# The fourth stage of a decoder kernel on one core: x added by TensorE and copied by ScalarE, three of sixteen triangles weighted on ScalarE, another order at the loop's ends

## What is computed

```python
phi = k_val[..., None] * theta                     # k_val (b, l, 32, 8), theta 8 values
re_k, im_k = (jnp.cos(phi), jnp.sin(phi))
merged = jnp.concatenate([p_w, pw5 * re_k, pw5 * im_k], axis=-1)    # p_w: a weight per head and row
cs = jnp.cumsum(merged, axis=1)                    # den, num_re, num_im
state_re, state_im = num_re / den, num_im / den    # inv_den = 1 / max(den, 1e-4)
out_re = jnp.sum(state_re * q_re + state_im * q_im, axis=-1)
out_im = jnp.sum(state_im * q_re - state_re * q_im, axis=-1)
y = out_re @ W_re + out_im @ W_im                  # per head, 8 -> 48
y = y_val * silu(y_gate)
x = x + y @ W_out
```

## Time and profile before

| what | value |
|---|---|
| median of three runs (lowest, highest) | 1734.25 us (1733.59, 1737.01) |
| profiled execution, its own time | 1731.17 us |
| its span, first to last instruction | 1729.4 us |
| mean granted TensorE clock | 0.965 of full speed |
| busy in the span: PE, PEld, DVE, ACT, POOL | 91%, 73%, 61%, 49%, 39% |
| the loop of the fourth stage | from 1028.2 us to 1332.7 us, 304.5 us |
| of it, steps 9 to 31, in which all parts run | from 1099.0 us |

### The profile page before, as it was taken

One profiled execution on the slowest core, in us unless ns is written; L12 is line 12 of the kernel. 1 busy time (PEld: TensorE's weight loads), 2 busy tenths in 40 slices (PEclk: granted clock), 3 DMA queues, 4 the chain that ended last, 5 costly groups with the idle time before them and its releaser, 6 DMA issues. The chain is left out here.

```text
span 1729.4 us, 37862 instructions
## 1 busy us (share of the span) xinstructions
PE 1577.0 (91%) x15048; PEld 1270.1 (73%) x15048; DVE 1056.8 (61%) x1671; ACT 849.3 (49%) x1466; POOL 678.7 (39%) x527
## 2 busy tenths in 40 slices
PE   6999999999997887898999787999996898999998
PEld 4788888888885665776888464666664675888887
DVE  5757666766666887676432659999994574111121
ACT  3545455545552665655422356667672674222222
POOL 0212212212222563531422256999994431223322
PEclk9999999999997997999999798999999898999999
DMA  3111201202113100001010120000001900000000
GB/s 106 37 45 53 80 27 52 79 27 67 63 46 114 58 2 26 10 12 23 26 68 39 44 49 2 1 2 2 2 2 39 359 10 1 1 13 13 1 12 13
DMA packets 72353, 70.29 MB, mean 41 GB/s; under 512 B 24816, under 2 KB 64368, under 8 KB 71840
## 3 DMA queue, kind: packets, MB, share of 16 engines
q1 hardware_dynamic: 72224, 68.46, 12.4%
HBM read 46.03 MB, written 19.27 MB: 38 GB/s over the span
## 5 line engine op out<-in xcount | busy, mean ns | idle before, releaser
L1503 DVE TENSOR_TENSOR s6f_hid<-s6f_act_sb,s6f_u_ps 128x512 f32<-128x512 f32 x64 | 44.0, 687 | 218.2 <-PE s6f_u_ps L1454 218.2
L1526 POOL TENSOR_TENSOR s6f_hid_parts<-s6f_hid,s6f_hid_parts 128x512 fp32r<-128x512 f32 x64 | 82.7, 1292 | 223.3 <-ACT s6f_hid_parts L1492 223.3
L712 DVE TENSOR_TENSOR x_rows<-x_rows,s_o_ps 128x1024 f32<-128x1024 f32 x64 | 78.0, 1219 | 135.2 <-PE s_o_ps L612 135.2
L2243 POOL TENSOR_TENSOR s4b_with_q<-s4b_with_q 128x1024 f32<-128x1024 f32 x64 | 150.9, 2384 | 0.9 <-DVE s4b_with_q L2198 0.9
L2198 DVE TENSOR_TENSOR s4b_with_q<-s4b_c_ps,s_q_rows 128x2048 f32<-128x2048 f32 x64 | 146.0, 2284 | 2.2 <-PE s4b_c_ps L2337 2.2
L667 ACT ACTIVATE s_zT<-s_z_ps,s_bias 128x512 fp32r<-128x512 f32 x64 | 44.1, 689 | 150.0 <-PE s_z_ps L603 150.0
L612 PE MATMUL s_o_ps<-s_w_parts,s_zT 128*128 128x256 f32 x768 | 110.1, 294 | 4.6 <-DVE s_zT L693 4.6
L2535 POOL TENSOR_TENSOR s1q_halves<-s1q_full,s1q_halves 128x768 fp32r<-128x768 f32 x16 | 33.3, 2084 | 200.6 <-ACT s1q_halves L2523 200.6
L1492 ACT ACTIVATE s6f_hid_parts<-s6f_hid 128x512 fp32r<-128x512 f32 x64 | 40.5, 632 | 143.8 <-PE s6f_o_ps L1474 140.5
L543 PE MATMUL s_v_ps<-s_wv_parts,s_xnT 128*128 128x256 f32 x768 | 104.0, 285 | 1.9 <-PEq L283 1.4
L1474 PEld LDWEIGHTS s6f_o_ps<-s6w_parts,s6f_hid_parts 128*128 128x128 f32 x768 | 99.1, 188 | 6.6 <-issue 1.0
(11 more groups left out here) (332 smaller groups left out, 3886.6 us busy)
## 6 DMA issues: line engine op xcount, KB each, us to landing
stored_weights<-s1q_halves SPq DMA_DIRECT2D x16, 768.0 KB, 3.9
s6w_parts<-stored_weights SPq DMA_DIRECT2D x32, 384.0 KB, 7.3
s1q_packed<-in_codes SPq DMA_DIRECT2D x8, 384.0 KB, 4.9
s1q_scale<-in_scale_rows SPq DMA_DIRECT2D x8, 384.0 KB, 5.4
s3p_raw<-in_ffn_pieces SPq DMA_DIRECT2D x8, 384.0 KB, 9.1
early_values<-s_vbd SPq DMA_DIRECT2D x1, 2176.0 KB, 12.0
s_vbd<-early_values SPq DMA_DIRECT2D x4, 544.0 KB, 7.2
x_rows<-in_x SPq DMA_DIRECT2D x4, 512.0 KB, 5.4
```

The costliest lines, as they stand in the source:

```text
L712: nc.vector.tensor_tensor(core.x[:, t0:t0 + TG, :], core.x[:, t0:t0 + TG, :], o_ps[:, :, :].rearrange("p b (t n) -> p (b t) n", t=2), ALU. ...
L1503: nc.vector.tensor_tensor(hid[:, f % 2, :], act_sb[:, f % 2, :], u_ps[:, f % 2, :], ALU.mult) \
L1526: nc.gpsimd.tensor_tensor(hid_parts[:, f % 2, 1, :], hid[:, f % 2, :], hid_parts[:, f % 2, 0, :], ALU.subtract).then_inc(low_done, 1)
L2243: nc.gpsimd.tensor_tensor(with_q[:, half, :, 0, :, n_, :], with_q[:, half, :, 0, :, n_, :], with_q[:, half, :, 1, :, 1 - n_, :], op).then_ ...
```

## The change

Within the steps in which all parts run:

- VectorE's `add` goes. TensorE's `output` now begins with a matmul of x with the identity, so that the sum of x and of the six old products stands in PSUM, and ScalarE's `write_back` copies it to x. It has lag 8 as `add` had; it stands in ScalarE's list behind `sines` and before `yT_copy`, and it now gives `added`.
- GpSimd weights 13 of the 16 triangles; the other three are three operations of ScalarE between the sine and the absolute value, with the weight as a scale read per row. `running_sums` waits for both.

At the ends: the reciprocal of `den` is taken in two halves in step 0 and not whole in step 1; a Silu of one column before the loop loads the table; for the first units `sines` stands before `rounding(0)`, and for units 2 and 3 `phases` and `fraction` stand behind the sums and the products. In the last steps VectorE takes the scaling of units 30 and 31, the subtraction and the product with the gate of unit 31. The last turns and outputs go to the free banks of `turns_ps` and `c_ps`, and their order is written out by hand.

```diff
@@ VectorE
+                        if isinstance(u, int) and u == 0:
+                            tiles = slice(n_ * NT // 2, (n_ + 1) * NT // 2)
+                            nc.vector.reciprocal(inv_den[:, tiles, :], den[:, tiles, :]).then_inc(inverted, 1)
...
-                run_steps(dve, UNITS, [(reduce, 4), (add, 8), (fraction(0), 0), (products(0), 2),
-                                       (fraction(1), 0), (products(1), 2), (gather_stats, 8)])
+                run_steps(dve, UNITS, [(within(LAST, UNITS, combine_last), 4), (reduce, 4),
+                                       (within(LAST - 1, UNITS, scale_late), 4), (within(LAST, UNITS, multiply_last), 5),
+                                       (within(0, 2, fraction(0)), 0), (within(4, UNITS, fraction(0)), 0),
+                                       (products(0), 2), (within(2, 4, fraction(0)), 0),
+                                       (within(0, 2, fraction(1)), 0), (within(4, UNITS, fraction(1)), 0),
+                                       (products(1), 2), (within(2, 4, fraction(1)), 0), (gather_stats, 8)])
@@ GpSimd
-                run_steps(pool, UNITS, [(multiply, 6), (scale, 5), (weight, 1), (combine, 3)])
+                run_steps(pool, UNITS, [(within(0, LAST, multiply), 6), (within(0, LAST - 1, scale), 5),
+                                        (weight, 1), (combine, 3)])
@@ ScalarE
+                def write_back(u, i, half):
+                    if half == 0:
+                        return
+                    act.wait_ge(o_full, i + 1)
+                    nc.scalar.activation(core.x[:, i, :], output_of(u, i), ACT.Copy).then_inc(added, 1)
...
+                    for k in range(OWN, HK):
+                        nc.scalar.activation(tri_p[:, half, k, :], tri_seq, ACT.Copy,
+                                             scale=p_rows[:, i, half * HK + k:half * HK + k + 1]) \
+                            .then_inc(weighted_here, 1)
...
+                nc.scalar.activation(afrac[:, 0:1], core.c("half_pi"), ACT.Silu)
+                run_steps(act, UNITS, [(within(0, LAST - 1, gates), 6), (within(0, 3, sines), 1), (rounding(0), 0),
+                                       (within(3, UNITS, sines), 1), (within(0, LAST - 3, write_back), 8), (within(0, LAST - 2, yT_copy), 6),
+                                       (within(0, LAST - 1, outT_copy), 5),
+                                       (rounding(1), 0), (cosines, 1)], head=UNITS + 8)
+                outT_copy(30, 15, 0)
+                gates(30, 15, 0)
+                yT_copy(29, 14, 1)
+                outT_copy(31, 15, 1)
+                gates(31, 15, 1)
+                yT_copy(30, 15, 0)
+                write_back(29, 14, 1)
+                yT_copy(31, 15, 1)
+                write_back(31, 15, 1)
@@ TensorE, turn_outs
-                    wait(pe, added, i - 1)
+                    wait(pe, added, min(i, LAST // 2 - 1) - 1)
@@ TensorE, output
+                    nc.tensor.matmul(output_of(u, i), core.c("ident"), core.x[:, i, :], start=True, stop=False)
                     for c in range(6):
-                        last = nc.tensor.matmul(o_ps[:, D:2 * D], yT[:, i % 2, c // 3, c % 3, :], w_out[:, c, :],
-                                                start=(c == 0), stop=(c == 5))
+                        last = nc.tensor.matmul(output_of(u, i), yT[:, i % 2, c // 3, c % 3, :], w_out[:, c, :],
+                                                start=False, stop=(c == 5))
```

More of the change, by code:

```diff
@@ L1808, in stage_L1_attention @@
     UNITS = 2 * NT
+    LAST = UNITS - 1
     ROUND = 12582912.0
@@ L2161, in upto, with within, guarded @@
                 return min(n, most) if isinstance(n, int) else n
+            def within(first, to, part):
+                def guarded(u, i, half):
+                    if (first <= u < to) if isinstance(u, int) else to - first > UNITS // 2:
+                        part(u, i, half)
+                return guarded
             def q_view(i, half):
@@ L2172, in by_bank, with turned_y, output_of @@
                 return rows.rearrange("p (a k) n -> p a k n", a=2)
+            def turned_y(u):
+                if isinstance(u, int) and u >= LAST - 2:
+                    return turns_ps[:, 0:3 * P]
+                return y_ps[:, 0, 0:3 * P]
+            def output_of(u, i):
+                if isinstance(u, int) and u >= LAST - 4:
+                    n = i - (LAST - 4) // 2
+                    return c_ps[:, n // 2, n % 2, 0:D]
+                return o_ps[:, D:2 * D]
             @block.vector
@@ L2234, in weight @@
                     nc.gpsimd.tensor_tensor(
[L2235 to L2237 removed]
+                        tri_p[:, half, 0:OWN, :], tri_seq.unsqueeze(1).to_broadcast([P, OWN, S]),
+                        p_rows[:, bass.ds(i, 1), half * HK:half * HK + OWN].rearrange("p t k -> p (t k)")
+                        .unsqueeze(2).to_broadcast([P, OWN, S]), ALU.mult).then_inc(weighted, 1)
                 def combine(u, i, half):
                     pool.wait_ge(prod_done, 2 * (u + 1))
[L2242 removed]
+                    last = isinstance(u, int) and u == LAST
+                    for n_, op in ((0, ALU.add), (1, ALU.subtract))[:1 if last else 2]:
                         nc.gpsimd.tensor_tensor(with_q[:, half, :, 0, :, n_, :], with_q[:, half, :, 0, :, n_, :],
@@ L2355, in heads @@
                     pe.wait_ge(oT_out, u + 1)
-                    wait(pe, yT_out, u)
+                    if u < LAST - 1:
+                        wait(pe, yT_out, u)
+                    else:
+                        pe.wait_ge(gated, u)
                     for part in range(2):
```

67 lines of the change are left out of this document (46 added, 21 removed).

## The result

| | before | after |
|---|---|---|
| median of the runs, us | 1733.92 (1733.47 to 1737.01, 4 runs) | 1771.09 (1770.82 to 1771.63, 4 runs) |
| profiled execution, its time and span, us | 1731.17, 1729.4 | 1771.09, 1769.3 |
| mean granted clock | 0.965 | 0.950 |
| first `phases` to the start of the next stage, us | 305.6 | 340.4 |

The change makes the kernel slower, clear of the noise: ratio 1.0196, 95% interval 1.0167 to 1.0225, so the loss lies between 1.7% and 2.2%. The prediction was 1763.8 us, range 1748 to 1778.

The account below looks back on a forecast made before the run. The prediction took a two-step ring of waits through TensorE, ScalarE and VectorE (16.90 us) as the bound. Terms 4.9 + 25.6 + 6.4 - 0.4 - 7.0 = +29.5 us gave 1760.7, plus 3.1 for the median: 1763.8 us, range 1748 to 1778.

Parts of the forecast that it names:

- The predicted ring: Closed chain of waits through TensorE, ScalarE and VectorE over two steps: 7.74 + 3.84 + 5.32 = 16.90 us before the change.
- The odd leg: Odd step, ScalarE's first rounding to VectorE's second fraction: from 3.84 to 5.97 us.
- term (3): Odd steps: write_back gives added, so TensorE waits for ScalarE's copy before turn_outs; +2.13 us each, 12 times, +25.6 us.
- Terms (1) to (3): Steady steps: x's matmul on TensorE +4.9 us; three triangles on ScalarE and its late copy together +25.6 us.
- w: Time of ScalarE's three triangles together in a step: 0.72 us, with ends at 0.16 and 1.20.
- Term (4): Steady steps: GpSimd saves 3/16 of each weighting and VectorE the add, neither on the ring: 0.
- Term (5): Granted clock falling after TensorE's new stand in odd steps: 4 falls of 1.6 us, +6.4 us, bounds 0 and 19.
- The ends: Loop's start -0.4 us (bounds -2 and +1); loop's end net -7.0 us (bounds -12 and -2).
- A: Faster: VectorE is the bound, a pair takes 16.1 us, 1717 us in all; 7%.
- B: No change: the wait is half as long and the ends give -12, 1734 us; 3%.
- C: Predicted chain with the clock kept, its term at 0: 1757 us; hardly a fall had 35%.
- D: Predicted chain with the clock down in every pair, its term at 19: 1777 us; most falling had 15%.

Follow-up runs that it names:

- e3: Changed kernel with ScalarE's copy of x at the head of its step and all 16 triangles on GpSimd; 1729.67 us.
- e1: Changed kernel with ScalarE's copy of x at the head of its step, before the first rounding; 1747.72 us.
- e2: Changed kernel with all 16 triangles weighted on GpSimd and none on ScalarE, copy of x left in place; 1748.87 us.
- e6: Changed kernel with ten unused matmuls on constants ahead of turn_outs in odd steps from the fifth on, to keep TensorE busy; 1755.63 us.
- e4: Changed kernel with only its new loop ends: VectorE adds x as before for tiles 0 to 12, all triangles on GpSimd; 1725.84 us.
- e13: Kernel of e4 with odd-step output between first phases and running sums, second phases and rounding earlier, and three triangles on ScalarE; 1723.49 us.
- e5: Changed kernel with six of 16 triangles weighted on ScalarE in place of three; 1786.68 us.

## Why the prediction was right, point by point

**The direction and the chain.** The predicted ring was right in each leg. The odd leg was to be 5.97 us and is 6.01; x's matmuls were to add 0.41 and add 0.44; the pair was to take 19.44 and takes 19.51 undisturbed. In the signs that the prediction named: the stand of 2 to 2.7 us in front of `turn_outs`, ended by the copy, is 2.23; VectorE's wait of over 2 us is 2.40; its share was to be 83%, and is 79% with the falls. One sign was off: from the reduction of unit 31 to the last statistics it was to be about 7 us shorter, and is 5.6 (20.0 to 14.4). e3 shows that nothing else of the moved work counts, and e1 and e2 that the two causes inside term (3) are 1.47 and 0.70 us.

**Terms (1) to (3).** 4.9 + 25.6 = 30.5 us predicted; 28.7 + 2.2 = 30.9 measured. w, which the trace of before did not show, was put at 0.72 us from the rows of operations with a scale from a tile, and the triangles' step is 1146.76 - 1146.04 = 0.72. The bounds of 0.16 and 1.20 were not needed. The Trainium skill's figure for a pointer operand ("ScalarE: Activation LUTs", What ACT_TABLE_LOAD costs), by which it would be the same 0.72, agrees with this row.

**Term (4)** was zero, and is: VectorE's busy time fell from 16.48 us a pair (164.83 / 10) to 16.21 (162.10 / 10) and GpSimd's from 16.24 to 15.49, and the pair did not heed it. The 16.59 us of the single pair at 1144.51 is no measure of it, since its stretch takes in 12 operations and the next one 11.

**Term (5), the clock, was mis-sized.** I took 4 falls of 1.6 us, 6.4. Four full ones between step 9 and step 31 cost 1.92 us each, and the first two pairs are 0.7 us long each, at a granted clock of 0.92. The fall in step 31 costs 1.15 in the odd leg and, by e6, 1.75 behind it. Together that is 7.7 + 1.4 + 1.15 + 1.75 = 12.0 us, the whole by which e6's stage is shorter. The price of one fall is 1.15 us in the odd leg (0.46 in `turn_outs`, where I had 0.2, and 0.69 in `phases`, as reckoned), 0.63 from the odd step's second fraction to the next (0.54 of it VectorE's wait for the sums; I had 0.7 for them), and 0.14 from there on, where TensorE comes late from the heads, which took 2.44 and not 1.56. The number of falls was a guess between none and all, and that four of the eleven pairs had a full one is luck. The runs show that falls go with the stand (e6) but not a rule by which I could have counted them.

**The ends.** -0.4 and -7.0 predicted; -0.6 and -5.7 measured in the changed kernel, -0.9 and -6.2 in e4. The first is smaller than what the clock does before step 9 (e3), so it neither confirms nor refutes the term. At full clock, by e6, the second is 5.7 + 1.75 = 7.45, close to 7.0, but by two misses that cancel, which is luck. From the last fraction to the scaling's end the time went from 32.04 us (1288.83 to 1320.87) to 26.52, and to 24.77 in e6: 7.3 less, where I had reckoned 8.7. The scaling gained its 5.2 + 0.2, and 1.0 came ahead of the combination (19.23 us before, 18.21 in e6), as reckoned. But from the combination's start to the reduction it is 3.81 us for 4.68, a gain of 0.9 and not 2.3: GpSimd's addition was done at 1357.35, but VectorE had first to scale unit 30 and began the subtraction at 1357.55. From the scaling's end on, the stage is 0.2 us shorter, where I had reckoned 1.7 longer. By these terms a tail as long as before gives -8.7, and the bound of -12 has no sum behind it.

**The sum.** +29.5 us predicted, +34.8 in the stage. Of the 5.3 missing, the clock is 5.6, terms (1) to (3) are 0.4, and the ends at full clock take off 0.6. The profiled execution is 39.9 us longer. 5.7 of that lie ahead of the stage, where the code is the same, -0.6 behind it. Kernels with the same code there began this stage between 1028.2 and 1038.8 us; I did not follow this up, and it may be why medians differ by 37.2 us and not by 34.8.

**The rivals.** A, VectorE as the bound (by the rule of the Trainium skill, "Perfetto Trace Analysis", Identifying the Most-Contended Engine, optimize the busiest engine first), did not come: e3 takes `add` off the busiest engine, has no late copy, and its pair is longer than before's. The rule did hold in e13, after the ring was opened; there the busiest engine has no pauses left. B needed ScalarE to reach the copy 2 us sooner, and the stand of 2.23 us shows that it did not. C, the chain with the clock kept, is what e6 shows apart from its extra matmuls: its stage is 22.8 us longer than before, against 29.5 - 6.4 = 23.1, and the kernel takes 1755.6 us against 1757. D, a fall in every pair, did not come in the changed kernel, but nearly in e5.
